# Recurrent attention layer with gated FFN on 8 cores: the token-major decayed keys are taken by transposing the feature-major keys

## What is computed

```
Q, K, V = heads(xn @ Wq + bq), heads(xn @ Wk + bk), heads(xn @ Wv + bv)   # 16 heads of 64
scores  = Q @ K.T / 8
mask    = where(i - j >= 0, 0.99 ** (i - j), 0)
r       = layernorm((scores * mask) @ V) * gamma + beta
s       = (r * sigmoid(xn @ Wg + bg)) @ Wo + bo
g       = silu(gelu(xn @ w1 + b1) @ w2 + b2)
out     = x + s * g
```

## Time and profile before

| | us |
|---|---|
| median of 2 runs | 1723.21 (1719.6 to 1726.83) |
| profiled execution | 1721.28 |
| span of its slowest core (core 7) | 1719.5 |
| spans of the 8 cores | 1704.3 to 1719.5 |
| mean granted TensorE clock, cores | 0.840 to 0.847 |

### The profile page before, as it was taken

One profiled execution on the slowest core, in us unless ns is written; L12 is line 12 of the kernel. 1 busy time (PEld: TensorE's weight loads), 2 busy tenths in 40 slices (PEclk: granted clock), 3 DMA queues, 4 the chain that ended last, 5 costly groups with the idle time before them and its releaser, 6 DMA issues.

```text
span 1719.5 us, 21166 instructions; the slowest of 8 cores (1704.3 to 1719.5 us)
## 1 busy us (share of the span) xinstructions
PE 1310.1 (76%) x7530; PEld 703.0 (41%) x7530; DVE 469.4 (27%) x1196; ACT 282.4 (16%) x594; POOL 147.1 (9%) x144
## 2 busy tenths in 40 slices
PE   0399947875476876886868868785599999999993
PEld 0034324532233333343333333431366666756661
DVE  0775021343044233332442433414000110011011
ACT  0022210100110211201101112021213131212120
POOL 0000000001001001001010010101002211221122
PEclk9999977786668677697686877966899999999997
DMA  8231047999500001001000000042502201220121
GB/s 157 98 123 50 1 98 106 113 113 116 93 1 25 25 1 38 13 1 49 1 25 25 1 13 13 1 171 98 208 1 75 74 28 47 75 72 21 56 75 37
DMA packets 16044, 100.41 MB, mean 58 GB/s; under 512 B 3397, under 2 KB 3782, under 8 KB 11974
## 3 DMA queue, kind: packets, MB, share of 16 engines
q0 software_dynamic: 6144, 44.06, 14.6%
q1 hardware_dynamic: 9654, 46.62, 8.2%
q10 hardware_dynamic: 144, 8.39, 1.4%
HBM read 109.56 MB, written 33.55 MB: 83 GB/s over the span
## 4 chain that ended last, share of the span: by engine, by line
PE 65%; DVE 14%; DMA 8%; issue 6%; ACT 3%; POOL 2%; DVEq 1%; SPq 0%; ACTq 0%; POOLq 0%
PE pY L1064 13%; PE pH L1040 9%; PE pPJ L557 7%; PE pPJ L519 4%; PE pS L789 3%; DMA s_scr<-WB 3%; PE pPJ L536 3%; PE pPJ L594 3%; PE pM L866 3%; PE pRT L644 2%; PE pRT L658 2%; PE pM L894 2%; DMA cpreS<-cpre 2%; DMA WB<-w2b 2%; DVE WB L629 2%
## 5 line engine op out<-in xcount | busy, mean ns | idle before, releaser
L1064 PE MATMUL pY<-WB,hT 128*128 128x512 bf16 x1024 | 225.5, 381 | 17.0 <-DMA WB<-w2b 17.0
L1040 PE MATMUL pH<-xnT,WB 128*128 128x256 bf16 x2048 | 227.5, 273 | 12.7 <-ACT hT L1050 11.7
L1040 PEld LDWEIGHTS pH<-xnT,WB 128*128 128x128 bf16 x2048 | 199.2, 98 | 42.5 <-issue 17.9
L789 PE MATMUL pS<-WB 128*128 128x512 bf16 x256 | 106.1, 538 | 127.0 <-POOL WB L779 66.2
L1064 PEld LDWEIGHTS pY<-WB,hT 128*128 128x128 bf16 x1024 | 100.6, 98 | 136.1 <-issue 19.8
L1094 DVE SCALAR_TENSOR_TENSOR xg<-pY,xg 128x1024 f32<-128x1024 f32 x16 | 19.6, 1224 | 470.7 <-ACT xg L1091 428.3
L1050 ACT ACTIVATE hT<-pH,b1Ts 128x256 bf16<-128x256 f32 x256 | 99.4, 481 | 226.1 <-PE pH L1040 226.1
L557 PE MATMUL pPJ<-xnT,WB 128*128 128x256 bf16 x1024 | 118.1, 276 | 13.0 <-DVE WB L548 12.3
L557 PEld LDWEIGHTS pPJ<-xnT,WB 128*128 128x128 bf16 x1024 | 93.6, 98 | 39.1 <-issue 17.1
L789 PEld LDWEIGHTS pS<-WB 128*128 128x128 bf16 x256 | 28.1, 116 | 196.6 <-issue 189.6
L629 DVE TENSOR_TENSOR WB<-pSCB,maskS 128x256 bf16<-128x256 f32 x64 | 27.1, 424 | 255.5 <-PE pSCA L623 252.1
(11 more groups left out here) (135 smaller groups left out, 1343.7 us busy)
## 6 DMA issues: line engine op xcount, KB each, us to landing
xg<-xpre SPq DMA_DIRECT2D x12, 1024.0 KB, 4.8
xg<-xseg SPq DMA_DIRECT2D x8, 1024.0 KB, 4.9
w1b<-w POOLq DMA_DIRECT2D x1, 8192.0 KB, 106.7
w2b<-w POOLq DMA_DIRECT2D x1, 8192.0 KB, 178.6
s_scr<-WB POOLq DMA_DIRECT2D x16, 512.0 KB, 3.0
xg<-xseg SPq DMA_DIRECT2D x16, 512.0 KB, 4.9
sld<-s_scr SPq DMA_DIRECT2D x16, 512.0 KB, 3.4
out<-sld POOLq DMA_DIRECT2D x16, 512.0 KB, 3.0
```

The source lines that it names most:

```text
L789: A("tensor", lambda e, it=it, dt=dt, ns=ns: e.matmul(pS[:, :], AsS[:, GRP * dt + 128 * it:GRP * dt + 128 * it + 128], WoS(1024 * dt + 512 ...
L1040: A("tensor", lambda e, dht=dht, dm=dm, sub=sub, pH=pH, gc=gc: e.matmul(pH[:, 256 * sub:256 * sub + 256], w1S(4096 * dm + 128 * dht, 128), ...
L1064: A("tensor", lambda e, lt=lt, dht=dht, ns=ns, it=it, pY=pY, half=half: e.matmul(pY[:, 512 * ns:512 * ns + 512], hT[:, 256 * lt + 128 * it ...
```

## The change

In `stageM1` the token-major K projection (L536, L543) and its eviction by VectorE (L548) are left out. After Q and K feature-major, `KuS` is now made from `KsS`: 16 transposes of 128 by 128 on TensorE, four at a time into `pSCA` and `pSCB` in turn (read there as bf16), and each four are evicted by ScalarE with the factor 0.99^256. Since `KsS` carries 0.99^(-i), this gives the key times 0.99^(256-i). The bias of K is in `KsS` already.

```diff
@@ stageM1
-                    for dm in range(NDM):
-                        for ns in range(2):
-                            A("tensor", lambda e, it=it, dm=dm, ns=ns, gc=gc: e.matmul(
-                                pPJ[:, 512 * ns:512 * ns + 512],
-                                xnT[:, 2048 * dm + gc + 128 * it:2048 * dm + gc + 128 * it + 128],
-                                WkS(1024 * dm + 512 * ns, 512),
-                                start=(dm == 0), stop=False, skip_group_check=True),
-                              reads=["xnT", "w.k"], writes=["p.PJ0", "p.PJ1"])
-                    for ns in range(2):
-                        A("tensor", lambda e, ns=ns: e.matmul(
-                            pPJ[:, 512 * ns:512 * ns + 512],
-                            orbS[0:1, :], bkB[0:1, 512 * ns:512 * ns + 512],
-                            start=False, stop=True, skip_group_check=True),
-                          reads=["c.orb", "r.bkB"], writes=["p.PJ0", "p.PJ1"])
-                    A("vector", lambda e, it=it: e.tensor_scalar(
-                        KuS[:, 1024 * it:1024 * it + 1024], pPJ[:, :],
-                        kusS[:, it:it + 1], None, ALU.mult),
-                      reads=["p.PJ0", "p.PJ1", "c.kus"], writes=["b.Ku"])
...
+                for it in range(2):
+                    for q in range(2):
+                        pT, pTtok = ((pTR2[:, 0:512], "p.SCA"),
+                                     (pSCBb[:, 0:512], "p.SCB"))[q]
+                        for hq in range(4):
+                            hp = 4 * q + hq
+                            A("tensor", lambda e, it=it, hp=hp, hq=hq, pT=pT: e.transpose(
+                                pT[:, 128 * hq:128 * hq + 128],
+                                KsS[:, 256 * hp + 128 * it:256 * hp + 128 * it + 128],
+                                identS[:, :]),
+                              reads=["b.Ks", "c.ident"], writes=[pTtok])
+                        A("scalar", lambda e, it=it, q=q, pT=pT: e.activation(
+                            KuS[:, 1024 * it + 512 * q:1024 * it + 512 * q + 512],
+                            pT[:, 0:512], AF.Identity, scale=float(D256)),
+                          reads=[pTtok], writes=["b.Ku"])
```

## The result

| | before | after |
|---|---|---|
| profiled execution, us | 1721.28 | 1664.76 |
| span of its slowest core (core 7), us | 1719.5 | 1663.2 |
| ratio of the runs after to before | | 0.9639, 95% interval 0.9586 to 0.9691 |
| granted TensorE clock, core 7 | 0.842 | 0.830 |

The change makes the kernel 3.6% faster. The medians of all runs (1675.21 of 11, 1729.5 of 10) hold executions in which the cores of one die showed a lower granted clock, and the ratio is of the runs without the slow ones among them. With it the 1723.21 of before become 1661, where the prediction was 1663. The gain is 62 us by the ratio (53 to 71), and the spans of the two profiled executions differ by 56.3 us.

A forecast was written before the change was run, and what follows sets the result against it. TensorE's order of work was taken to set the time. Over six of eight groups, 68.3 + 3.4 + 3.3 - 15.5 = 59.5 us saved gave 1663 us; forecast 1650 to 1675 (0.74), full range 1642 to 1685.

The forecast's parts named there:

- Removed blocks and the clock in `stageM1`: `stageM1`, six groups: 12 K blocks of 5.69 us go, 68.3 us; full clock saves 3.4 (second V) and 3.3 (feature-major).
- The first two groups: M1(0) and M1(1): some 26 us removed, 5 added, both ending in the `stageL(0)` wait, growing from 34.6 to about 55.
- The addition: End of `stageM1`: 16 transposes and 4 evictions cost 2.5 us in five groups, 3.0 in M1(7); 15.5 us taken.
- The eviction: ScalarE's scaled copy of 512 columns from PSUM takes 0.60 us each, with no table load added.
- Rival B: Evictions at the end of `stageM1` need their own table: two loads a group, 15 us, 1678 us; chance 0.06.
- Rival A: M1(0) and M1(1) count too, the `stageL(0)` wait ending earlier: 21 us more gain, 1642 us; chance 0.08.
- Rival D: `stageM1`: second V and whole feature-major block at 1.2 GHz, 17.7 us a group, 1768 us, slower; chance 0.02.
- Rival C: Low clock into `stageL` and gate projection, or at first V blocks: 2 to 4 us a group, 1675 to 1687; chance 0.10.

## Why the prediction was right

- **Removed blocks and the clock in `stageM1`**: 68.3 + 3.4 us forecast up to the feature-major block, 72.5 measured. The feature-major blocks lost the 3.3 us of their slow forms as well. That the clock depended on the wait for VectorE was inferred from few rows; the run with the scaling on ScalarE shows it at the place. One of the rows was weak: the mean of 454 ns of L519 also holds the first V blocks, which follow no wait and ran partly at the low clock as well (4.26 us in M1(3) above, 3.63 in M1(7)).
- **The first two groups**: forecast to end in the wait, which should grow to about 55 us. It grew to 57.6: 20.6 us of saving, where 26 - 5 = 21 were forecast, and 2.4 of a later landing. Four runs show the cause.
- **The addition**: 15.5 us forecast, 18.6 measured (15.3 + 3.3), 3.1 us a group in place of 2.5. The schedule up to the transposes of `stageE_fin` came out nearly as worked out: first four 15.05 us into the feature-major block in both, `stageE_fin` 2.82 us behind it where 2.69 were forecast. The mis-sized part is behind that: 3.23 us to L753 where 2.76 were forecast, with those transposes at 0.58 us and not 0.38, that is at 1.2 GHz. The prediction had this as a bound and not in its value. In M1(7), where no `stageE_fin` follows, 3.0 were forecast and 3.1 measured.
- **The eviction**: 0.60 us taken, 597 ns measured. By the rule of the Trainium skill ("ScalarE: Activation LUTs", section "Table sets: the hidden batching unit") Identity needs no table load of its own; the two loads in the groups of the changed kernel agree. Rival B falls.
- **Not forecast**: the start of `stageL` takes 4.3 us more, and the Wo products 6.0 less. Both are stretches at another clock, and that they nearly cancel is luck. The 6.0 do not need the shorter `stageM1` beside them, since the kernel with only groups 0 and 1 changed has them too (139.3 us); their cause stays open.
- **Rival A** (the first two groups count) is refuted as the kernel stands and right once the conversion is moved. **Rival D** did not occur: no V or feature-major block behind a wait for ScalarE ran at the low clock in any group on any core.
- **Rival C** was right that `stageL` starts colder, by 0.9 us in most groups. Counted over eight cores, behind M1(1) to M1(6), a start is cold here when its first pair of matmuls (L753, L756 of before) takes over 1 us:

| kernel | cold starts of 48 |
|---|---|
| before | 4 |
| before, w2 later | 0 |
| before, scaling on ScalarE | 27 |
| changed | 48 |
| changed, transposes in the gate projection | 42 |
| the same, w2 later | 45 |
| the same, w2 later and V in halves | 21 |

The transposes of K at the end of `stageM1` are not needed for it (42), nor is a shorter `stageM1` (27 with all four blocks in place), and the shortest `stageM1` of all has fewer (21). The last two lines differ by the two waits of 1.25 us in each `stageM1`, so these waits, or the 2.2 us that went with them, have a part in it, as rival C supposed of small waits. The rest of the cause stays open.

The sum of 59.5 us came to 56.3: 0.8 more from the blocks up to the feature-major one, 3.1 less for the addition, 1.7 more from the two clock effects in `stageL`, 2.4 less for the later end of the wait, and 0.2 less in the rest of the table. Each term that was forecast came about by the mechanism given for it; that the total is only 3.2 us off is helped by errors that run against each other.

## What to carry to other kernels

Before counting a saving in every iteration, look for a wait downstream whose end is fixed by something that the saving does not move; here an 8 MB transfer issued once, ahead in the same queue as a small store, swallowed some 20 of 80 us, and moving it in the changed kernel was worth nearly as much as the change (55.3 against 56.3 us on core 7). A cheap operation added where an engine hands over costs the pace of the slowest engine in the exchange, not its own length: 16 transposes of 0.06 us cost 3.1 us at the end of a stage and about 1.0 us between matmuls that were running anyway. A PSUM tensor that is waited for whole cost its eviction each time here, and filling and copying it by halves removed that wait.

## What was not expected of the hardware

A wait of 1.54 us between blocks of matmuls was followed by a stretch at 1.2 GHz in 28 of the 64 second V blocks (eight groups, eight cores); waits of 1.25 and 1.36 us ahead of the same blocks never were, in 64 each. And the first pair of matmuls of `stageL` was at the low clock (1.22 us against 0.69 to 0.86) in 4 of 48 starts before and in all 48 after; neither the length of `stageM1` nor the transposes ahead of it decide that alone.
